# Post-norm transformer pair on one core: the first eight heads' maxima in runs of four over six banks, and another order of the last feed-forward networks

## The reference

```python
x = _layernorm(x + _L0_attn_ref(x, L0_attn_Wqkv, L0_attn_bqkv, L0_attn_Wproj, L0_attn_bproj), axis=-1)
x = _layernorm(x + _L0_ffn_ref(x, L0_ffn_W_exp, L0_ffn_b_exp, L0_ffn_up_weights, L0_ffn_up_bias, L0_ffn_down_weights, L0_ffn_W_con, L0_ffn_b_con, L0_ffn_down_bias), axis=-1)
x = _layernorm(x + _L1_attn_ref(x, L1_attn_Wqa, L1_attn_Wqb, L1_attn_Wkva, L1_attn_Wkvb, L1_attn_Wout, L1_attn_bout), axis=-1)
x = _layernorm(x + _L1_ffn_ref(x, L1_ffn_w_gate, L1_ffn_w_up, L1_ffn_w_down), axis=-1)
```

## Time and profile before

| | |
|---|---|
| median of 3 runs | 374.52 us (372.81 to 375.2) |
| the profiled execution | 375.42 us, its span 373.5 us |
| TensorE busy | 340.0 us (91%) |
| VectorE busy | 250.9 us (67%) |
| ScalarE busy | 189.2 us (51%) |
| GpSimd busy | 178.1 us (48%) |
| mean granted clock of TensorE | 0.965 |

### The profile page before, as it was taken

How to read it: one execution, slowest core, us unless ns; L and a number is a source line. 1 busy time by engine, 2 the same in 40 slices (tenths; PEclk the granted TensorE clock), 3 DMA queues, 4 the chain that set the end, 5 groups by cost and what they waited for, 6 DMA issues and landing times.

```text
span 373.5 us, 10260 instructions
## 1 busy us (share of the span) xinstructions
PE 340.0 (91%) x3804; PEld 234.7 (63%) x3804; DVE 250.9 (67%) x940; ACT 189.2 (51%) x397; POOL 178.1 (48%) x299
## 2 busy tenths in 40 slices
PE   7879999999999999999999699898999999999672
PEld 3546766666657656576657566586777767676452
DVE  3444667586866777586866668486888898964533
ACT  2123755745585655836575445744556555545100
POOL 5664072140300706046352967339695954637420
PEclk9696999999999999999999989999999999999968
DMA  7321522110011001200202011110112110000000
GB/s 262 125 92 66 75 71 79 31 31 2 3 32 30 4 1 31 47 16 17 46 14 44 4 31 29 33 30 3 32 45 48 29 40 10 18 3 16 16 14 14
DMA packets 9469, 14.27 MB, mean 38 GB/s; under 512 B 2140, under 2 KB 5196, under 8 KB 9292
## 3 DMA queue, kind: packets, MB, share of 16 engines
q1 hardware_dynamic: 8828, 12.83, 13.5%
q10 hardware_dynamic: 592, 0.79, 0.7%
HBM read 6.28 MB, written 1.05 MB: 20 GB/s over the span
## 4 chain that ended last, share of the span: by engine, by line
PE 73%; POOL 9%; issue 6%; ACT 5%; DVE 5%; ACTq 1%; POOLq 0%; DVEq 0%
PE SM L342 26%; PE G L524 10%; PE ST L361 6%; PE G L435 5%; PE G L448 4%; PE G L498 4%; PE G L424 3%; PE G L457 2%; PE G L415 2%; PE G L506 2%; POOL ln_f L834 2%; ACT L580 1%; PE G L468 1%; POOL xb L924 1%; PE ST L392 1%
## 5 line engine op out<-in xcount | busy, mean ns | idle before, releaser
L580 ACT ACTIVATE E<-ST 128x512 f32<-128x512 f32 (+1 forms) x256 | 125.3, 541 | 126.5 <-PE ST L361 126.4
L342 PE MATMUL SM<-QK 31*128 31x256 f32 (+1 forms) x1024 | 146.6, 384 | 8.0 <-ACT QK L610 4.2
L361 PE MATMUL ST<-QK 32*128 32x256 f32 (+1 forms) x1024 | 137.6, 379 | 4.4 <-ACT E L580 4.4
L342 PEld LDWEIGHTS SM<-QK 31*128 31x128 f32 x1024 | 97.7, 189 | 49.0 <-DVE mx L708 13.3
L708 DVE TENSOR_REDUCE mx<-SM 128x2 f32<-128x512 f32 x128 | 82.2, 685 | 44.0 <-PE SM L342 43.6
L361 PEld LDWEIGHTS ST<-QK 32*128 32x128 f32 x1024 | 92.1, 187 | 8.0 <-ACT E L580 6.5
L716 DVE CUSTOM_DVE_ANT_0 masked_s<-SM,mask_sb 128x256 f32<-128x256 f32 (+1 forms) x256 | 75.7, 351 | 23.9 <-PE SM L342 23.3
L885 POOL TENSOR_TENSOR at<-turned,rec 128x256 f32<-128x256 f32 x16 | 10.1, 628 | 94.9 <-DVE rec L726 94.9
L524 PE MATMUL G<-E,V 128*32 128x256 f32 x992 | 53.6, 356 | 0.5 <-POOL E L878 0.5
L878 POOL TENSOR_SCALAR_AFFINE_SELECT E<-E 128x512 f32<-128x512 f32 x64 | 39.0, 634 | 14.0 <-ACT E L580 14.0
L524 PEld LDWEIGHTS G<-E,V 128*32 128x32 f32 x992 | 28.6, 109 | 22.4 <-issue 8.0
(11 more groups left out here) (130 smaller groups left out, 427.5 us busy)
## 6 DMA issues: line engine op xcount, KB each, us to landing
QK<-qk SPq DMA_DIRECT2D x56, 64.0 KB
rs<-ry SPq DMA_DIRECT2D x16, 128.0 KB, 2.3
xb<-x_nat SPq DMA_DIRECT2D x1, 1024.0 KB, 4.8
out<-ln_g SPq DMA_DIRECT2D x8, 128.0 KB, 1.9
xt<-x_t SPq DMA_DIRECT2D x1, 896.0 KB, 6.7
wi<-wi_all SPq DMA_DIRECT2D x1, 576.0 KB, 3.8
QK<-mt SPq DMA_DIRECT2D x32, 8.0 KB
fac<-fac_u SPq DMA_DIRECT2D x1, 508.0 KB, 6.4
```

Of the source, the lines that this page charges most:

```text
L342: ins = nc.tensor.matmul(SM[m % S_RING][:, cols], q, QK[rows, b % QK_RING, r, 1, keys], start=True, stop=True)
L361: ins = nc.tensor.matmul(ST[m % S_RING][:, c * T:(c + 1) * T - q0], QK[rows, b % QK_RING, r, 1, c * P:(c + 1) * P], QK[rows, b % QK_RING, ...
L580: act.activation(E[:, a % E_RING, j, 0:n], ST[m % S_RING][:, 0:n], ACT.Exp, scale=SCALE)\
```

## The change

- **Start.** Queries and keys of the groups 0 and 1 are projected first (`project_group`), the keys of group 0 into the bank `ST2`, so that VectorE adds their bias while ScalarE copies the queries. The maxima of heads 0 to 7 then come in two runs of four heads over the six banks `SM` and `ST`; the projections of groups 2 and 3 follow. VectorE does the eight reductions in a row, and ScalarE all copies of the four groups, ahead of the loop. The loop starts at step -6 instead of -44, with fillers for six heads instead of eight, batch 1's projection at -6 instead of -10, and the values of batch 0 at -4 instead of -8. The transfers of batch 1 move from ScalarE's queue to SyncE's.
- **End.** For batch 14 (the last FFN but one) the third up projection and its tanh move from step 268 to 264 (`LAST_UP1`), ahead of the attention projection at 266; VectorE's gating is done at 262, 264 and 268 (`LAST_GATED`) instead of 258, 262 and 268. `normalise_last` moves from step 266 to 268, behind the third gating. The last attention pair waits for half of its mask first, and the last down projection for two of three chunks first.

```diff
...
+LAST_UP1, LAST_GATED = (34, 38, 40), (38, 40, 44)
...
-FIRST, FINAL = AT_QK[2], HEADS + 44
...
+AHEAD = 2 * STRIPS
+FIRST, FINAL = AHEAD - LEAD, HEADS + 44
...
-FIRST_AT, EARLY, FILL = (FIRST, -12, -8, -4), (None, -10, 2), 8
+EARLY, EARLY_V, FILL = (None, FIRST, 2), FIRST + 2, 6
...
-            if b is not None and b % 2 == parity:
+            if b and b % 2 == parity:
...
+def up1_at(g, c, last=LAST_UP1):
+
+    b = batch_at(g, AT_UP1[c], (1,))
+    return BATCHES - 2 if g - last[c] == H * (BATCHES - 2) else b if b != BATCHES - 2 else None
...
+        keys_bank = ST[S_RING - 1]
+
+        def max_bank(m):
+
+            return (SM + ST)[m % (2 * S_RING)] if m < AHEAD else SM[m % S_RING]
...
-                if b is not None and b != 1:
+                if b is not None:
...
+            def project_group(r):
+
+                bank = claim(("first", r), first_out, 2 * r + 1)
...
+                for s in range(2):
+
+                    to = keys_bank if r == 0 and s == 1 else bank
+                    ins = nc.tensor.matmul(to[:, s * T:(s + 1) * T], wfirst_sb[:, r, s, :], xt[:, 0:T], start=True, stop=True)
+                ins.then_inc(first_ps, 1)
...
-                        pe.wait_ge(first_out, 2 * (r + 1))
+                        pe.wait_ge(first_out, 2 * r + 1)
+                        if r == 0:
+                            pe.wait_ge(first_keys, 1)
...
-                    if m >= S_RING:
+                    if m >= AHEAD:
                         pe.wait_ge(A["max_done"], m - S_RING + 1)
+                    elif m >= 2 * S_RING:
+                        pe.wait_ge(A["max_done"], m - 2 * S_RING + 1)
...
+                if c == 0:
+                    if m == -FILL:
+                        pe.wait_ge(A["max_done"], 2 * S_RING)
+                    elif m >= S_RING - FILL:
+                        pe.wait_ge(filled, m + FILL - S_RING + 1)
...
+            project_group(0)
+            project_group(1)
+            for r in range(2):
+                for c in (1, 0):
+                    for m in range(STRIPS * r, STRIPS * (r + 1)):
+                        max_scores(m, c)
+            project_group(2)
+            project_group(3)
...
-                    pe.wait_ge(F1["hid_ready"], SC * (i + 1))
+                    pe.wait_ge(F1["hid_ready"], SC * (i + 1) - (1 if b == BATCHES - 1 else 0))
...
                         for c in range(SC):
+                            if q == 0 and c == SC - 1 and b == BATCHES - 1:
+                                pe.wait_ge(F1["hid_ready"], SC * (i + 1))
...
-                        pe.wait_ge(A["masked"], 4 * (n - 2 * NB + 1))
+                        pe.wait_ge(A["masked"], 4 * (n - 2 * NB + 1) - (2 if n == 2 * BATCHES - 1 else 0))
...
+                        if e == 1 and n == 2 * BATCHES - 1:
+                            pe.wait_ge(A["masked"], 4 * (n - 2 * NB + 1))
...
+            for r in range(GROUPS):
+                act.wait_ge(first_ps, r + 1)
+                if r == 0:
+                    act.wait_ge(ld["first"], 32)
+                for s in range(1 if r == 0 else 2):
+                    act.activation(QK[:, 0, r, s, :], g_bank["first", r][:, s * T:(s + 1) * T], ACT.Identity,
+                                   bias=bfirst_sb[:, r, s:s + 1]).then_inc(first_out, 1)
...
-                        if b == 1:
-                            act.wait_ge(A["qk_out"], 2)
-                            act.wait_ge(zeros_ready, 1)
-                            for j in range(STRIPS):
-                                act.dma_start(QK[STRIP * j:STRIP * j + ROWS, 1, :, :, :], qk[j:P:STRIPS, 1, :, :]).then_inc(qk_in[1], 16)
...
+            dve.wait_ge(first_ps, 1)
+            dve.wait_ge(ld["first"], 32)
+            nc.vector.tensor_scalar(QK[:, 0, 0, 1, :], keys_bank[:, T:2 * T], bfirst_sb[:, 0, 1:2], None, ALU.add)\
+                .then_inc(first_keys, 1)
+            for m in range(AHEAD):
+                maximum(m)
...
-                    if (b := batch_at(g, AT_UP1[c], (1,))) is not None:
+                    if (b := up1_at(g, c, LAST_GATED)) is not None:
...
+                if g == H * (BATCHES - 1) + AT_LN:
+                    b = BATCHES - 1
+                    dve.wait_ge(last_ready, 1)
+                    dve.wait_ge(A["xt_ps"], b - 1)
+                    dve.wait_ge(F1["res_done"], b - NB - 1)
+                    normalise_last(NA, b % 2, A["ln_ready"])
...
```

86 lines of the change are left out of this document (34 added, 52 removed).

## The result

The changed kernel takes **364.22 us** (median of 4 runs, 363.05 to 366.05), the kernel before 374.59 us beside it (4 runs, 372.81 to 375.2): a ratio of 0.9735, with a 95% interval of 0.9683 to 0.9787. The forecast was 362.0, with a range of 359.0 to 367.0. The profiled execution took 364.26 us; its span is 362.2 us, against 373.5 before, so 11.3 us shorter.

What follows compares the result with a forecast made beforehand. The prediction took TensorE's own work to bound the middle, leaving gains at the two ends: 10.2 + 2.2 + 0.5 = 12.9 us. From 375.42 or the median that gave 362.5 or 361.6; forecast 362.0, range 359.0 to 367.0.

Steps and rivals of the forecast that it cites:

- the front: Start of the kernel up to step 4: reordered at full clock, step 4 starts at 26.1 instead of 36.27, gain 10.2 us.
- the middle: Rival, from step 4 on: a late load or GpSimd's sums stall TensorE and take time back; 364 to 369 us, chance 0.12.
- the end: Batch 14's up to down projection gains 2.2 us, att comes 0.45 earlier, last down projection's split wait gains 0.5.
- Reductions and banks: Start: VectorE's eight reductions run without idle time from 9.7 to 14.9, two projections under them end at 14.1.
- Steps to the first exponential scores: Start: steps -6 to 0 follow, step 0 starts at 21.3, exponentials' matmuls near 21.9 against 29.52 before.
- About 1.9 per pair: Start, from step -2: steps go by VectorE's pace, about 1.9 us per pair of reductions.
- With 2 us to land: Batch 1's four loads on SyncE's queue, issued by 20.4, land at 22.4 before head 16 at 23.3; cost 0, up to 1.
- The cold stretch in front: Rival, start: the clock still falls once or twice, 3.0 us each, giving 365.0 or 368.0; chance 0.32.
- I take 0, since a wait of that size remains: End: a shorter TensorE wait might keep the clock up, worth up to 1.6 us more; counted as 0.
- The distance from the first exponential score to att, 322.2 before, 3 to 4 us shorter: Test mark: 3.0 of clock and 0.45 at the end shorten this distance; otherwise the prediction would be wrong.
- slower: Rival, step 2: batch 1's loads land late and hold TensorE; the slowest early landing would cost 4, giving 366; chance 0.02.
- no wait for a load at head 16: Sign, start: TensorE does not wait for batch 1's loads when it reaches head 16.

Runs made afterwards that it cites:

- three_banks: Changed kernel with the first eight heads' maxima in the three SM banks only, in runs of two heads; 368.46 us, ratio 0.9818 to the kernel before.
- b1_two: Changed kernel with batch 1 projected ahead of step -6, two of its four loads issued before the first maxima's load, two behind; 360.77 us, ratio 0.9633.
- changed_again: The changed kernel itself, unaltered, run again on another occasion; 364.24 us, ratio 0.9724 to the kernel before.
- b1_early: Changed kernel with batch 1 projected ahead of step -6 and its four loads issued ahead of the first maxima's load; 362.71 us, ratio 0.9677.
- front_only: Changed kernel with its end put back as before, so only the new start; 370.24 us, ratio 0.9843 to the kernel before.
- end_only: Kernel before with only the changed end; 370.96 us, ratio 0.9893 to the kernel before.
- xb_later: Changed kernel with the 1024 KB load of xb moved from first to fourth place of the late loads; 368.13 us, ratio 0.9798.
- no_fill: Changed kernel without any filler matmuls; 363.46 us, ratio 0.9685 to the kernel before.
- undo_gate: Changed kernel with VectorE's gating of batch 14's first two chunks back at steps 258 and 262; 366.97 us, one execution.
- b1_act: Changed kernel with batch 1's four loads back on ScalarE's queue, the xb load staying on SyncE's; 367.80 us, ratio 0.9799.
- b1_early_mt: Changed kernel with batch 1 projected ahead of step -6, its four loads issued behind the first maxima's load; 365.22 us, ratio 0.9712.
- undo_norm: Changed kernel with the last attention's normalisation back ahead of the third gating; 368.74 us, one execution.

## Why the prediction was right, and which steps were off

**The time.** 364.22 lies in the range and 2.2 us above the forecast of 362.0. The sum of 12.9 was 1.6 above the measured 11.3. Its parts missed by more: the front gave 1.6 less than forecast, the middle took 1.6, and the end gave 1.55 more. That the total came this near is in part luck, since the end's surplus is mostly the clock's, and the same program places its falls elsewhere in the next execution.

- **Reductions and banks: right.** Forecast: no idle time from 9.7 to 14.9; measured 9.74 to 14.62. The two projections lie under them (12.14 to 14.13, forecast 14.1), step −6 starts at 14.21 (14.2 to 15.3). In three_banks' profile the reductions end 1.6 us later and the first copy of maxima comes 5.7 later, at most 3.4 of it by the clock.
- **Steps to the first exponential scores: 1.7 too late.** Forecast near 21.9, measured 20.19. Step −4 starts at 16.46, not 17.0, step −2 at 18.18, not 18.9, and step 0 at 19.34, not 21.3; its second head and the exponential scores are held to 20.09 and 20.19, where a bank comes free. From the start of step −2 to these scores it is 2.0 us, and I had given it 3.0. "About 1.9 per pair" is no steady pace: the pairs of reductions start at 15.37, 17.62, 19.34 and 21.74, so 2.25, 1.72 and 2.40 apart.
- **"With 2 us to land": the step that failed.** I reckoned by the size of one load and left out that four stand in a row. The maxima's load of 8 KB alone did land in 1.7 us, but the last of the four landed 3.9 us behind the end of its issue (20.07 to 23.99; TensorE goes on at 24.04). My upper bound of 3.9 from the earlier trace rows was the right value, and the price named with it, "up to 1", was too small, because TensorE was ready for head 16 at 22.38 instead of 23.3 and its clock fell at the end of the wait. Here 1.66 of wait and the half clock to 27.2 stood in place of 0: step 4 at 27.85 instead of 26.1, a gain of 8.4 instead of 10.2. b1_two shows the term's full size: there step 4 starts at 24.53.
- **The cold stretch in front was a rival (0.32, 3.0 us each), and half came.** There is one of 3.4 us in the changed profile and of 6.8 in changed_again, both behind the wait for batch 1. Such a stretch of 3.4 us costs 1.6 (17.04 − 15.40 below), half of the 3.0 assumed for 6 to 7. The row it named for the second fall before, 28 to 30 us with 1.66 of 2.00, is not the thin one; that is 26 to 28, with 1.07. The rival did not name the wait as a cause; with the wait gone the stretch is gone too in b1_two's profile, but b1_early, with its wait of 0.74 us up to 20.84, has one of 3.4.
- **The middle took 1.6 back, which I had given 0.12 as a load or GpSimd being late.** It was neither. The same work between copies 21 and 22 takes 15.40 us in before, front_only, end_only, xb_later, three_banks and changed_again, 15.39 in no_fill and undo_gate, and 16.98 to 17.04 in changed, b1_act, b1_early, b1_early_mt, undo_norm and b1_two. All of them have the same pause of TensorE, 1.5 us long, 5.5 us behind copy 21; in the second set alone the clock falls behind it. The changed kernel:

```profile
232.00:234.00 2.00, 0.50 (x10) 0.10 (x7) 0.34 (x1) 1.97 (x4) 0.00 (x0) 1.00 0.06 5
236.00:238.00 2.00, 2.00 (x10) 1.91 (x10) 1.01 (x3) 0.38 (x1) 1.75 (x3) 0.50 0.58 135
```

The kernel before, the same work 8 us later:

```profile
240.00:242.00 2.00, 1.14 (x22) 0.45 (x13) 0.45 (x1) 1.98 (x2) 0.00 (x0) 1.00 0.24 33
244.00:246.00 2.00, 2.00 (x17) 1.92 (x17) 1.70 (x9) 0.73 (x2) 1.06 (x2) 1.00 0.59 139
```

The pause is there in both (the first row of each fence), the clock is 0.50 behind it in one and 1.00 in the other. What decides it no run here settles: changed and changed_again are one program and differ in it (17.04 and 15.40, as the theory of changed_again allowed; its rival, the same places every time, falls).
- **The end: 2.2 measured 2.36, 0.45 measured 0.65, 0.5 measured 0.51.** Up to down projection is 7.64 instead of 10.0, so 2.36, of which the earlier att is 0.65 (the forecast had 1.9 to the down projection's start and 2.2 for the step in all). att follows `at` at once (345.63, 345.66). From the last `hid` to r_g it is 1.25 us instead of 1.76 (355.63 to 356.88; 366.42 to 368.18), 0.51. With as much time at half clock behind copy 31 as before (b1_act, 6.8), the new end takes 37.84 us instead of 40.73: 2.9, where 2.7 was forecast.
- **"I take 0, since a wait of that size remains": the second step that failed, and the bound of 1.6 too.** The wait of 2.17 us ahead of the down projection remained, but the clock stayed up behind it: 1.58 us for the 12 matmuls, 1.10 for the up projection. The same program from att to the end takes 16.5 us with the clock up (changed) and 19.5 with 6.8 us at half (b1_act and b1_early_mt, behind a wait of 2.18 and 2.17): 3.0 us, not 1.6. Of these, 1.6 were lost again by a fall at 334.4, ahead of att, which before did not have. So the part behind copy 31 is 2.9 + 3.0 − 1.6 = 4.3. Which way the clock goes is not fixed by the wait: in undo_gate, too, a wait of 2.17 ends in a fall, in undo_norm one of 3.90.
- **"The distance from the first exponential score to att, 322.2 before, 3 to 4 us shorter": it came out longer, 325.5** (20.19 to 345.66). By that mark the prediction would have been wrong. Against the 318.7 of the forecast (322.2 less 3.5) it has 3.5 more in front (the first score came 1.7 early and step 4 1.75 late), 1.6 in the middle and 1.4 behind copy 31, where the clock falls near 334 (19.94 us from copy 31 to att, 18.98 before, in spite of the earlier gating): 325.2. The mark was ill chosen, since the clock's falls move with the front.

The rival "slower" had its price about right: a wait for batch 1 of 5.07 us (b1_act) leaves 367.8, far below 374.6. Of the marks named, `att` came 0.03 behind `at` and the wait ahead of the down projection was 2.17 (2.4 forecast); "no wait for a load at head 16" failed.

## What to carry to other kernels

Write down, for each load that a moved start brings nearer, when it is issued, when it is needed, what stands ahead of it in its queue, and how long the last of such a group takes to land in the trace. Here a wait of 1.7 us came with a clock at half behind it, and b1_two, which has neither, is 3.5 us faster. When two groups of small loads share a queue and each has a deadline, try splitting the larger one around the smaller. And put a large load behind small urgent ones in the same queue; ahead of them on another it cost 3.4 us of waiting here.

## What the runs showed of the hardware

- Of four loads of 64 KB from SBUF to SBUF in a row, the last landed 3.0 to 3.9 us behind the end of its issue (before, changed, xb_later, b1_early, b1_two), whether 1024 KB followed in the same queue or not. With 1024 KB started ahead on another queue it was 6.2 us, and TensorE waited 3.4 us longer (b1_act). A load of 8 KB landed 1.7 us behind the start of its issue with nothing just ahead of it (changed), 3.7 behind the four (b1_early).
- One program, the same instructions, and the granted clock at different places: changed and changed_again have 3.4 and 6.8 us at half clock in front, 6.8 and 3.4 in the middle. A stretch of 15.40 us takes 17.04 with a fall in it. A wait of 2.17 us ahead of the same matmuls is followed by full clock in changed and by half clock in b1_early_mt and undo_gate. The Trainium skill, "TensorE: Matmul & The Clock Gate", Part 1, says that the throttled clock is the default and activity releases it; the traces agree in that every fall in these profiles has a pause of TensorE in the five us ahead of it, but the pause can be as short as 0.57 us (at 331 in changed), and the same pause does not always bring a fall.
- So a change that shifts the whole program by some us can win or lose 1.6 us in a stretch that it does not touch. In a comparison of two kernels the marks that both share tell such a term from the change's own.
